# Splitting the first-layer expert weights once, keeping all second-layer weights on chip, and routing a batch one stage earlier

## What is computed

```
q, k, v = split(x @ W_qkv)                  # 16 heads of 64
q, k = relu(q @ W_f + b_f), relu(k @ W_f + b_f)
kv = k.T @ v; out = (q @ kv) / (q . sum(k) + 1e-6)
x = layernorm(x + out @ W_out + b_out)
probs = softmax(x @ gate_w.T); p, e = top_k(probs, 2)
h = gelu(x @ w1[e] + b1[e])                 # 128 -> 512, for both experts of a token
y = h @ w2[e] + b2[e]                       # 512 -> 128
x = layernorm(x + sum over the two experts of p * y)
```

## Time and profile before

| | |
|---|---|
| median of 3 runs | 466.5 us (465.53 to 467.39) |
| profiled execution | 467.53 us, its span 465.7 us |
| TensorE busy | 435.6 us, 94% |
| TensorE loading weights | 344.6 us, 74% |
| VectorE busy | 302.6 us, 65% |
| ScalarE busy | 272.3 us, 58% |
| GpSimd busy | 162.2 us, 35% |
| DMA | 52.19 MB, 112 GB/s over the span |
| chain that ended last | TensorE 89%, VectorE 4%, DMA 3% |

### The profile page before, as it was taken

The page is one execution under the profiler, slowest core; times in us unless marked ns, Lnnn a source line. Parts: engine busy times, 40 slices in busy tenths (PEclk is TensorE's granted clock), DMA queues, the critical chain, the costliest instruction groups (busy, mean ns, idle before and its releaser), DMA issues.

```text
span 465.7 us, 8129 instructions
## 1 busy us (share of the span) xinstructions
PE 435.6 (94%) x2608; PEld 344.6 (74%) x2608; DVE 302.6 (65%) x899; ACT 272.3 (58%) x530; POOL 162.2 (35%) x164
## 2 busy tenths in 40 slices
PE   3999999999999999999999998999999999999940
PEld 2777776776776776776676675599999999999930
DVE  3383866986986976975975999665643222245784
ACT  2555656666665665665665663377555555555672
POOL 2101101112422421421421433067776555555550
PEclk9999999999999999999999999999999999999995
DMA  8920000000000000000000000788886987799343
GB/s 221 334 82 0 3 0 1 0 7 17 26 13 12 23 14 13 23 14 12 25 18 7 23 20 30 257 246 247 256 273 223 309 242 228 241 354 301 124 130 113
DMA packets 34442, 52.19 MB, mean 112 GB/s; under 512 B 4943, under 2 KB 24788, under 8 KB 34272
## 3 DMA queue, kind: packets, MB, share of 16 engines
q1 hardware_dynamic: 25136, 40.72, 28.5%
q0 software_dynamic: 4544, 8.54, 5.2%
q10 hardware_dynamic: 4720, 2.42, 1.8%
HBM read 39.82 MB, written 12.75 MB: 113 GB/s over the span
## 4 chain that ended last, share of the span: by engine, by line
PE 89%; DVE 4%; DMA 3%; issue 1%; ACT 1%; ACTq 1%; POOL 0%; POOLq 0%; SPq 0%; DVEq 0%
PE psA L640 14%; PE psO L532 12%; PE psG L649 9%; PE psA L434 6%; PE psA L436 6%; PE psA L435 6%; PE psS L649 6%; PE psA L511 6%; PE psG L523 3%; PE psG L554 3%; PE psG L434 3%; PE psG L435 3%; PE psA L579 3%; PE psG L436 3%; DMA bf_col<-bf 2%; PE psS L470 1%
## 5 line engine op out<-in xcount | busy, mean ns | idle before, releaser
L390 POOL DMA_INDIRECT expert_rows<-rows,pos x64 | 62.4, 976 | 114.2 <-DVE pos L1023 92.5
L415 POOL DMA_INDIRECT expert_results<-q_act,kT x56 | 55.2, 986 | 37.2 <-DVE q_act L1140 25.2
L668 ACT ACTIVATE kT<-psA,bf_col 128x512 f32<-128x512 f32 x64 | 43.9, 686 | 37.5 <-PE psA L436 37.2
L532 PE MATMUL psO<-qn,mixed 128*128 128x512 f32 x128 | 65.5, 598 | 0.0
L668 ACT ACTIVATE q_act<-psA,bf_col 128x512 f32<-128x512 f32 x64 | 43.9, 689 | 26.2 <-PE psA L436 26.1
L1054 DVE TENSOR_TENSOR qn<-q_act,psG 128x512 f32<-128x512 f32 x64 | 42.7, 680 | 5.3 <-PE psG L523 5.3
L819 DVE TENSOR_TENSOR k_lo<-psA,k_hi 128x512 fp32r<-128x512 f32 x64 | 43.5, 683 | 3.2 <-ACT k_hi L668 2.6
L511 PEld LDWEIGHTS psA<-cst,kT 128*128 128x128 f32 x256 | 31.1, 141 | 14.6 <-ACT kT L668 7.2
L434 PE MATMUL psA<-xT_hi,wk_hi 128*128 128x512 f32 x64 | 41.7, 652 | 0.0
L793 ACT ACTIVATE q_act<-psA,xT_raw 128x256 f32<-128x256 f32 x84 | 34.5, 470 | 10.7 <-PE psA L640 10.1
L511 PE MATMUL psA<-cst,kT 128*128 128x128 f32 x256 | 38.6, 273 | 1.5 <-DVE k_lo L819 1.5
(11 more groups left out here) (180 smaller groups left out, 903.1 us busy)
## 6 DMA issues: line engine op xcount, KB each, us to landing
xT_raw<-w SPq DMA_DIRECT2D x21, 578.0 KB, 4.6
x_raw<-w SPq DMA_DIRECT2D x18, 578.0 KB, 4.8
...
xT_raw<-xT SPq DMA_DIRECT2D x1, 1792.0 KB, 10.7
...
```

Of the source, the lines that this page charges most:

```text
L390: pool.indirect_dma_start(xs, bass.IndirectOffsetOnAxis(ap=pos_2[o % 2][:, j, k:k + 1], axis=0), rows_2[o % 2][:, j, k, :], None).then_inc ...
L415: pool.indirect_dma_start(ys, bass.IndirectOffsetOnAxis(ap=xrow[r][:, c, D:D + 1].bitcast(I32), axis=0), yrow[u][:, c, :], None, bounds_ch ...
L532: mm(psO[:, :], mixed[:, c, :], qn[:, c % 4, :], start=c == 0, stop=c == CH - 1).then_inc(o_pe, 1)
L668: return act.activation(out_, in_, func, **kw)
```

## The change

- **First-layer weights.** SyncE loads w1 of each expert once. ScalarE and VectorE split it into a high and a low part, in the key loop of stages 1 (two experts) to 7 (`SPLIT_AT`), and SyncE writes both to a DRAM tensor `expert_weights`, beside b1 and b2 that are copied there. In the expert part a block loads one piece of 1156 columns from there (w1 high and low, b1, b2), into eight slots in the space of `k_hi`, `k_lo` and `w_more`.
- **First layer.** It is `three` products in float32r, of the split weights and of rows that are split as well: VectorE writes a low part `xT_lo`, and TensorE waits for that (`e_Tl`) in place of the high part.
- **Second-layer weights.** All eight are loaded once into `x_raw`, when the last batch has been split; TensorE reads the number of the block's expert from the table (`choose`) and takes the weights at an offset worked out from it.
- **Routing.** In stage b the router works on batch b-1, in the second half: pick and mark behind the logits, weigh and place behind the reciprocals. All pieces of a batch are scattered in one stage. The early table moves into the key loop of stage 7, on a buffer of its own (`past`).
- **Start.** Ten products on zeros come first on TensorE. `bf_col` and the identity are loaded ahead of the other constants. The query fold and the mean of the gate weights move into the key loop of batch 0, and with them the work of the other engines on them.
- **End.** The step numbers of fetch, means, chain and norm are new.

```diff
-FETCH = {31: 0, 32: 1, 33: 2, 34: 3, 37: 4, 38: 5}
-STAT_AT = {31: 0, 32: 1, 33: 2, 35: 3, 37: 4, 38: 5, 40: 6}
-CHAIN_AT = {36: (0, 4), 39: (4, 6), 40: (6, 7)}
-NORM_AT = {37: 0, 38: 1, 39: 2}
+FETCH = {30: 0, 31: 1, 33: 2, 34: 3, 37: 4, 38: 5}
+STAT_AT = {30: 0, 32: 1, 34: 2, 36: 3, 38: 4, 39: 5, 40: 6}
+CHAIN_AT = {37: ((0, 4),), 40: ((4, 6), (6, 7))}
+NORM_AT = {38: 0}
...
-W_ROW = F + FC + FC * D + D
+W_ROW = 2 * F + FC + D
+SPLIT_AT = {1: ((0, 2), (1, 5)), **{b: ((b, 3),) for b in range(2, B)}}
+W_SLOTS = 8
...
+        wb = nc.dram_tensor("expert_weights", [E, P, W_ROW], F32, kind="Internal").ap()
...
+        w_more = sb("w_more", [P, 2 * W_ROW], F32R)
+        w1_raw = [sb(f"w1_raw{i}", [P, F])[:, :] for i in range(2)]
+        w1_split = [w_more[:, 2 * F * i:2 * F * (i + 1)] for i in range(2)]
...
+        past = [sb(f"past{i}", [1, LATE * len(ERAS) * E]) for i in range(2)]
...
-        past = [qn_space[0:1, a * 704:(a + 1) * 704] for a in range(2)]
-        rows_T = r_rest[:, :]
...
-        w_raw = [xT_raw[:, u * W_ROW:(u + 1) * W_ROW] for u in range(3)] + [
-            x_raw[:, :, :].rearrange("p c d -> p (c d)")[:, u * W_ROW:(u + 1) * W_ROW] for u in range(SLOTS - 3)]
-        w2_raw = [w[:, F + FC:W_ROW - D].rearrange("p (c n) -> p c n", c=FC) for w in w_raw]
-        b2_bc = [w[:, None, W_ROW - D:].broadcast_to([P, 2, D]) for w in w_raw]
+        w1_slot = [space[:, u * W_ROW:(u + 1) * W_ROW] for space, fit in (
+            (k_hi[:, :, :].rearrange("p t n -> p (t n)"), 3), (k_lo[:, :, :].rearrange("p t n -> p (t n)"), 3), (w_more[:, :], W_SLOTS - 6)) for u in range(fit)]
+        w_raw = [w.bitcast(F32) for w in w1_slot]
+        b2_bc = [w[:, None, 2 * F + FC:].broadcast_to([P, 2, D]) for w in w_raw]
+        w2_all = x_raw[:, :, :].rearrange("p c d -> p (c d)")
...
+            def load_w1(ex):
+                sp.dma_start(w1_raw[ex % 2], w12[ex, :, 0:F]).then_inc(in_w1[ex % 2], 16)
+
+            sp.dma_start(wb[:, :, 2 * F:2 * F + FC], w12[:, :, F:F + FC]).then_inc(wb_in, 16)
+            sp.dma_start(wb[:, :, 2 * F + FC:], w12[:, :, F + FC + FC * D:]).then_inc(wb_in, 16)
+            load_w1(0)
+            load_w1(1)
+            for ex in range(E):
+                sp.wait_ge(w1_l, ex + 1)
+                sp.dma_start(wb[ex, :, 0:2 * F], w1_split[ex % 2].bitcast(F32)).then_inc(w1_out[ex % 2], 16)
+                if ex + 2 < E:
+                    load_w1(ex + 2)
+            sp.wait_ge(x_l, B)
+            sp.wait_ge(x_h, B)
+            sp.dma_start(w2_all.rearrange("p (e n) -> p e n", e=E), w12[:, :, F + FC:F + FC + FC * D].rearrange("e p n -> p e n")).then_inc(w2_in, 16)
+            sp.wait_ge(wb_in, 32)
+            for which in w1_out:
+                sp.wait_ge(which, 16 * E // 2)
+            sp.wait_ge(g_pe, 2 * B)
+
             def load_weights(n):
                 expert = sp.value_load(tabi[0:1, 0, n:n + 1], min_val=0, max_val=E - 1)
-                sp.dma_start(w_raw[n % SLOTS], w12[ds(expert, 1), :, :].rearrange("a p n -> (a p) n")).then_inc(e_w[n % SLOTS], 16)
+                if n >= W_SLOTS:
+                    sp.wait_ge(e_y, n - W_SLOTS + 1)
+                sp.dma_start(w_raw[n % W_SLOTS], wb[ds(expert, 1), :, :].rearrange("a p n -> (a p) n")).then_inc(e_w[n % W_SLOTS], 16)
 
             def load_rows(n):
                 first = sp.value_load(tabi[0:1, 1, n:n + 1], min_val=0, max_val=NOWHERE)
                 sp.dma_start(xrow[n % ROW_SLOTS], xs[ds(first, BLK), :].rearrange("(c p) d -> p c d", p=P)).then_inc(e_x[n % ROW_SLOTS], 16)
 
             sp.wait_ge(table, 2)
+            sp.wait_ge(r_l, B)
             for which in scattered_2:
                 sp.wait_ge(which, 16 * TILES * TOPK * SAFE // 2)
-            for n in range(SLOTS):
+            for n in range(W_SLOTS):
...
+                if n == 7:
+                    sp.wait_ge(e_T, 1)
...
-            for n in range(SLOTS, NBLK):
+            for n in range(W_SLOTS, NBLK):
...
-                sp.wait_ge(e_y, n - SLOTS + 1)
...
-                if 3 <= b < B:
-                    scatter(b - 3, range(TILES, PIECES))
                 if b >= 2:
                     scatter(b - 2, range(TILES))
-                if b == B - 1:
-                    pool.wait_ge(g_pe, 2 * b + 1)
+                    if b < B:
+                        pool.wait_ge(q_pe, CH * b + 1)
+                    else:
+                        pool.wait_ge(o_pe, CH * (b - 1) + 4)
...
-            pool.wait_ge(e_T, 4)
-            scatter(B - 2, (TILES, TILES + 1))
             for n in range(NBLK):
-                if 1 <= n < 3:
-                    scatter(B - 2, (TILES + 1 + n,))
...
+            pe.wait_ge(zero_ready, 1)
+            for _ in range(10):
+                mm(psS[:, 0:P], zeros[:, 0, 0:P], zeros[:, 0, 0:P], start=True, stop=True)
...
-            pe.wait_ge(in_c, 16)
-            pe.wait_ge(in_small, 64)
-            mm(psS[:, 0:E], con("ones"), gw[:, :], start=True, stop=True).then_inc(mean_pe, 1)
-            pe.wait_ge(in_fold_q, 16)
-            for c in range(CH):
-                last = mm(psG[:, c // 4, c % 4 * P:(c % 4 + 1) * P], wqkvT_sb[:, c, :], wfd[:, :], start=True, stop=True)
-            last.then_inc(fold_pe, 1)
+
+            def fold_queries():
+
+                pe.wait_ge(in_fold_q, 16)
+                for c in range(CH):
+                    last = mm(psG[:, c // 4, c % 4 * P:(c % 4 + 1) * P], wqkvT_sb[:, c, :], wfd[:, :], start=True, stop=True)
+                last.then_inc(fold_pe, 1)
+
+            def gate_mean():
+
+                pe.wait_ge(in_c, 16)
+                pe.wait_ge(in_small, 32)
+                mm(psS[:, 0:E], con("ones"), gw[:, :], start=True, stop=True).then_inc(mean_pe, 1)
...
+                    if b == 0 and c == 2:
+                        fold_queries()
+                    if b == 0 and c == 3:
+                        gate_mean()
...
-                if old:
-                    ranks(o)
...
+                    if prev:
+                        ranks(p)
...
-                    pe.wait_ge(e_Th, before(n))
+                    pe.wait_ge(e_Tl, before(n))
...
+            def choose(n):
+
+                if n == 0:
+                    pe.wait_ge(w2_in, 16)
+                if n in (0, EARLY):
+                    pe.wait_ge(table, 2 if n == 0 else 4)
+                return pe.value_load(tabi[0:1, 0, n:n + 1], min_val=0, max_val=E - 1)
...
-                u = n % SLOTS
-                pe.wait_ge(e_Th, n + 1)
-                pe.wait_ge(e_w[u], 16 * (n // SLOTS) + 16)
+                u = n % W_SLOTS
+                pe.wait_ge(e_Tl, n + 1)
+                pe.wait_ge(e_w[u], 16 * (n // W_SLOTS) + 16)
...
-                    mm(psH[v][:, c, :], w_raw[u][:, c * P:(c + 1) * P], rows_T[:, at], start=True, stop=True).then_inc(e_up, 1)
-
-            def second_layer(n):
+                    three(psH[v][:, c, :], w1_slot[u][:, c * P:(c + 1) * P], w1_slot[u][:, F + c * P:F + (c + 1) * P],
+                          xT_hi[:, at], xT_lo[:, at]).then_inc(e_up, 1)
+
+            def second_layer(n, expert):
...
-                        last = mm(psY2[bank_of(n)][:, t, :], hT[v][:, c, t * P:(t + 1) * P], w2_raw[n % SLOTS][:, c, :], start=c == 0, stop=c == FC - 1)
+                        last = mm(psY2[bank_of(n)][:, t, :], hT[v][:, c, t * P:(t + 1) * P], w2_all[:, ds(expert * (FC * D) + c * D, D)], start=c == 0, stop=c == FC - 1)
...
-                    second_layer(n - 2)
+                    second_layer(n - 2, expert)
+                if 1 <= n <= NBLK:
+                    expert = choose(n - 1)
...
-            act.dma_start(cst[:, :], consts[:, 0:_C["spread"][0]]).then_inc(in_c, 16)
+            for r in (0, DH):
+                act.dma_start(bf_col[r:r + DH, :], bf.rearrange("(d a) -> d a", a=1)).then_inc(in_bf, 16)
+            act.dma_start(cst[:, 0:P], consts[:, 0:P]).then_inc(in_ident, 16)
+            act.dma_start(cst[:, P:], consts[:, P:_C["spread"][0]]).then_inc(in_c, 16)
             act.dma_start(gw[:, :], gwT).then_inc(in_small, 16)
             act.dma_start(bout_col[:, :], bout.rearrange("(d a) -> d a", a=1)).then_inc(in_small, 16)
-            act.dma_start(bf_col[0:DH, :], bf.rearrange("(d a) -> d a", a=1)).then_inc(in_small, 16)
-            act.dma_start(bf_col[DH:P, :], bf.rearrange("(d a) -> d a", a=1)).then_inc(in_small, 16)
...
-                    if old and c == 3:
-                        exponents(o)
-                    if old and c == 6:
-                        fill(o)
+                    for ex, at in SPLIT_AT.get(b, ()):
+                        if c == at:
+                            act.wait_ge(in_w1[ex % 2], 16 * (ex // 2 + 1))
+                            if ex >= 2:
+                                act.wait_ge(w1_out[ex % 2], 16 * (ex // 2))
+                            hi(w1_split[ex % 2][:, 0:F], w1_raw[ex % 2]).then_inc(w1_h, 1)
+                    if b == 0 and c == 4:
+                        act.wait_ge(fold_pe, 3)
```

(44 more changed lines are left out.)

69 lines of the change are left out of this document (39 added, 30 removed).

## The result

The changed kernel takes 462.23 us (median of 4 runs, 461.57 to 462.59) beside 466.72 (4 runs) of the kernel before: ratio 0.9904, 95% interval 0.9888 to 0.9921. It is 4.5 us faster; 14 were forecast. The time lies outside the forecast's own range of 447 to 457 and inside the wide one of 446 to 465. In the profiled executions 467.53 became 462.59, the span 465.7 became 460.8.

A forecast was written before the change was run, and what follows sets the result against it. TensorE was taken to bound both parts, so a column saved there is time saved. Terms -6.0 + 0 + 2.4 - 0.3 - 12.5 + 1.8 + 0 = -14.6 gave 452.5 us, own range 447 to 457, wide range 446 to 465.

The forecast's parts named there:

- Head, -6.0: Kernel start: earlier bias DMA and keys ahead of the query fold start kT 7.0 us earlier, net -6.0 (-4.0 to -7.5).
- I take 1.0 us of the 7.0 back: Key loop of the head: with the query fold inside, it loses 1.0 of the 7.0 us that kT gains.
- Stages 1 to 6, 0: Attention stages: expert splits replace router steps in the key loop, the router moves under cover; 0 (0 to +1 each).
- Stage 7, +2.4: Stage 7's key loop: the table adds VectorE work, +3.97; less 1.2 slack and 0.3 given back, +2.4 (0 to +4).
- 1.2 us is slack: Stage 7: last qn done at 269.94, its output product starts at 271.17, so 1.2 us of added VectorE work is hidden.
- Expert pitch, -12.5: Expert first layer: 12 float32r products replace 4 float32 ones, saving 0.32 us in each of 39 blocks, -12.5 (-11.3 to -15.2).
- the fixed-extra end of the bounds: Expert first layer: 0.120 us per 256-column product if the 13 ns extra is fixed, 0.113 if it goes with columns.
- Expert stops, +1.8: Expert blocks: TensorE waits for VectorE's low part of the rows, +1.0 at the fourth block, +0.8 later; +1.8 (+0.5 to +4).
- Rival D: Expert part: DMA or VectorE binds, 0.1 to 0.25 us a block returns, 457 to 462 us; chance 0.11.
- DMA, 0: Expert part: the same weight bytes in a shorter block cost nothing, eight slots taking up the load; 0 (to +3).
- Register, 0: Expert part: TensorE's read of the block's expert and four offsets costs 0; bound from above 1.6 us, room 1.5 a block.
- Rival C: Expert first layer: float32r weight loads bind at 0.19 us a product, +34, about 487 us; chance 0.04.

The follow-up runs named there:

- e6: The changed kernel with the query fold and the split of its result moved behind the last key of the loop: 463.58 us, ratio 0.9926 to the kernel before.
- e2: The changed kernel with the low part of the next block's rows made earlier, right behind the result of block n-2: 460.20 us, ratio 0.9845 to the kernel before.
- e3: The changed kernel with the early table taken out of stage 7's key loop, three parts ahead of the means, two in stage 8: 459.98 us, ratio 0.9863.
- e4: The changed kernel with TensorE's register work doubled, the block's expert read twice and offsets worked out for each half: 463.44 us, ratio 0.9911.
- e8: The changed kernel with ScalarE's high part of the next batch's tokens ahead of the first norm, so GpSimd's subtraction comes earlier: 459.98 us, ratio 0.9853.
- e5: The changed kernel with the small DMAs for gate weights and output bias issued behind the copies that split the key weights: 461.09 us, ratio 0.9883.
- e7: The changed kernel without the ten products on zeros at its start: 463.20 us, ratio 0.9913 to the kernel before.
- e9: The changed kernel with e2's edit and the last batch's scatter pieces issued two to a block: 483.82 us, ratio 1.0027; the kernel before took 482.4 there.
- e18: The kernel before itself, unchanged, run again for its profile in the last set, where the kernel before took 485.2 us: 484.30 us, ratio 0.9991.

## Why the prediction was wrong

Of the 14.6 us forecast the profile has 4.9. Four rows of the table fall short, by 10.4 us together: the head by 3.7, stages 1 to 6 by 1.2, stage 7 by 1.6 and the experts by 3.9; the two others came out 0.4 and 0.3 better.

**Head, -6.0.** Two steps failed. "The second half then goes out at about 2.85 [...] so kT starts at about 10.7" left out ScalarE's own queue: the two issues behind took 2.87 us in place of 0.9 and put kT at 12.17, 1.5 late. The bias was in at 9.6, sooner than forecast; what failed is "split of weights and rows to about 9.5", which was done at 11.6. "I take 1.0 us of the 7.0 back" failed by more: the loop gave back 4.1, of which 1.3 to 2.0 is the fold (e6) and 0.6 to 1.3 the clock in that profile (against e2, e3, e4 and e8). The rest, some 1.5 us by e6, is not shown apart; e5 points to a loop whose start waits for identity and constants. Behind the loop 0.8 came back. The zeros I counted at nothing, "since the bias lands last". It does not land last, and without them kT is 0.7 and the first mixing product 0.9 to 2.4 us later (e7): without their gain the head would have gained less still.

**Stages 1 to 6, 0.** The key phase fell from 19.68 to 19.40 us, the second half rose from 14.85 to 15.15: the router's steps moved at no net cost, as predicted. What the forecast lacked is the meeting with GpSimd, 0.4 us in each of stages 2 and 5 (e8), and the 0.3 of stage 1, which had no router in its key loop to lose.

**Stage 7, +2.4.** "1.2 us is slack" was read from the chain qn to output. The k_lo of the same loop had next to none: in the kernel before the last k_lo started at 19.78 us of the stage, beside the first query product at 19.68, and the next turned keys wait for the bank that k_lo reads. From its timelines:

```profile
271.57 0.79 PE L434 MATMUL psA<-xT_hi,wq_hi 128*128 128x512 f32 x1
```

```profile
271.67 0.68 DVE L819 TENSOR_TENSOR k_lo<-psA,k_hi 128x512 fp32r<-128x512 f32 x1
```

So the last k_lo moved back by 3.9 and the key phase grew by 3.7, nearly all of the added 3.97 (3.94 by the forecast's own terms). The end of the stage, which was to give 0.3 back, took 0.3 more, as in every stage, and together it is 4.0 (e3).

**Expert pitch, -12.5.** Right in its mechanism and nearly in size: 12 products at 0.119, the fixed-extra end of the bounds (0.120), pitch 3.43 in place of 3.41; 38 x 0.30 = 11.4 is the fall between first and last second layer without the stops. By the Trainium skill ("TensorE: Matmul & The Clock Gate", Back-to-back issue gap) a product of 256 columns takes an estimated 109 ns; for float32r the trace's 119 are the better guide.

**Expert stops, +1.8.** 4.65 were measured. The step "it bites where VectorE has more" was right, its sizes were not: 1.24 for 1.0 at the first, and 3.4 for 0.8 elsewhere, because the stop of a low part that is late repeats at each means, and because the rows of the last batch were not looked at. e2 shows that order alone removes nearly all of what VectorE causes. Rival D names this ("the low parts come late in more blocks", 457 to 462), and at 0.1 us a block it is in part what happened; that the time came out beside it is luck, for more than half of what is missing stands ahead of the experts.

**DMA, 0** held at 467 us: share 1.00 and 0.92 in the two stretches and no wait for weights. In e9 to e18 it is the stores that seem to be late, a term that the forecast does not have. **Register, 0** is shown by e4, with 0.66 us of sequencer work a block where 1.6 was the bound. Rival C is refuted by the pitch.
